# One block with the second experts' weights and twelve tiles' rows ahead, and logits with the gate as stationary operand

## The reference

```python
# layer 0 attention: Sim = e.w1 + d.w2 + (e*w3) d^T, softmax, and
#   hcq = concat(e, hq_hat, e*hq_hat, e*hc_hat) @ W_qv + b_qv
# layer 0 experts (8 of width 512, and 4 that give x back), on the normalised rows
logits = einsum('btd,ed->bte', x, gate_w) + expert_bias     # 12 experts
topk_logits, topk_idx = top_k(logits, 2);  topk_w = softmax(topk_logits)
h = silu(x @ w1[e].T);  y = h @ w2[e].T                     # per expert
# layer 1 attention: 4 heads of 64, softmax(q k^T * scale) v, @ Wo
# layer 1 experts (8 of width 1024)
logits = xf @ Wg                                            # 8 experts
comb = one_hot(top_idx) * softmax(top_vals) * alpha
y = gelu(layernorm(xf)*ln_w[e]+ln_b[e] @ fc1_w[e] + fc1_b[e]) @ fc2_w[e] + fc2_b[e]
```

## Time and profile before

| what | value |
|---|---|
| median of 3 runs | 962.05 us |
| the profiled execution, its own time | 967.79 us |
| its span, first to last instruction | 965.9 us |
| mean granted TensorE clock | 0.956 |
| TensorE busy | 894.5 us (93%) |
| VectorE, ScalarE, GpSimd busy | 562.0, 491.3, 431.3 us |
| DMA | 134.72 MB, mean 139 GB/s |

### The profile page before, as it was taken

How to read it: one execution, slowest core, us unless ns; L and a number is a source line. 1 busy time by engine, 2 the same in 40 slices (tenths; PEclk the granted TensorE clock), 3 DMA queues, 4 the chain that set the end, 5 groups by cost and what they waited for, 6 DMA issues and landing times. The chain is left out here.

```text
span 965.9 us, 19473 instructions
## 1 busy us (share of the span) xinstructions
PE 894.5 (93%) x6189; PEld 766.2 (79%) x6190; DVE 562.0 (58%) x1286; ACT 491.3 (51%) x1044; POOL 431.3 (45%) x374
## 2 busy tenths in 40 slices
PE   6899999868999998779999999988899999999995
PEld 4798989746899996557777777757499999999995
DVE  7875453485566675666566575554764454454452
ACT  5744141354444553475665665545655455455552
POOL 2474341004555573755363462300255555555543
PEclk9999999978999999789999999985999999999998
DMA  9721000275766746611010100019667666676662
GB/s 306 239 95 44 1 1 1 76 248 187 254 228 232 253 157 221 135 44 44 5 63 22 45 1 2 28 52 353 229 184 195 211 200 190 209 203 187 206 198 28
DMA packets 68593, 134.72 MB, mean 139 GB/s; under 512 B 8080, under 2 KB 50704, under 8 KB 63408
## 3 DMA queue, kind: packets, MB, share of 16 engines
q1 hardware_dynamic: 55184, 110.27, 33.4%
q0 software_dynamic: 13344, 23.63, 11.2%
HBM read 109.08 MB, written 21.64 MB: 135 GB/s over the span
## 5 line engine op out<-in xcount | busy, mean ns | idle before, releaser
L1901 PEld LDWEIGHTS d_hps<-d_xg_t,d_xw 128*128 128x128 f32 x1248 | 145.2, 192 | 2.4 <-DVE d_xg_t L2085 1.0
L1799 ACT ACTIVATE x<-d_hps,b 128x128 f32<-128x128 f32 x312 | 89.3, 368 | 113.1 <-PE d_hps L1901 112.9
L1901 PE MATMUL d_hps<-d_xg_t,d_xw 128*128 128x128 f32 x1248 | 145.5, 275 | 0.8 <-DVE d_xg_t L2085 0.8
L883 POOL TENSOR_SCALAR c_prob<-c_prob,c_rinv 128x1024 f32<-128x1024 f32 x64 | 72.4, 1150 | 109.4 <-DVE c_rinv L1338 109.0
L1911 PE MATMUL d_yps<-d_w,d_hid_hi 128*128 x312 | 115.2, 402 | 0.0
L1704 POOL DMA_INDIRECT out_x<-d_y,d_take_slot x39 | 63.1, 1619 | 99.1 <-DVE d_y L2122 89.6
L1331 DVE CUSTOM_DVE_ANT_0 c_prob<-c_sc,c_minf 128x1024 f32<-128x1024 f32 x64 | 75.8, 1221 | 36.6 <-PE c_sc L976 34.4
L2085 DVE TENSOR_SCALAR d_xg_t<-d_take,ln_w,ln_b 128x128 f32<-128x128 f32 x78 | 28.5, 406 | 93.4 <-PE d_take L1890 93.1
L1914 PE MATMUL d_yps<-d_w,d_hid_lo 128*128 x312 | 81.2, 281 | 0.0
L1901 PEld LDWEIGHTS b_hps<-b_xg_t,b_w 128*128 128x128 f32 x624 | 76.7, 195 | 3.6 <-issue 1.9
L989 PE MATMUL c_tp<-const,c_prob 128*128 128x128 f32 x512 | 70.5, 281 | 9.8 <-DVE c_pt L1343 5.2
(11 more groups left out here) (367 smaller groups left out, 2106.6 us busy)
## 6 DMA issues: line engine op xcount, KB each, us to landing
d_xw<-in_w SPq DMA_DIRECT2D x39, 1024.0 KB
b_w<-in_w SPq DMA_DIRECT2D x47, 512.0 KB, 7.6
d_w<-in_w SPq DMA_DIRECT2D x8, 1024.0 KB, 12.3
a_raw<-in_ctx_t SPq DMA_DIRECT2D x8, 512.0 KB, 7.0
a_raw<-in_ctx SPq DMA_DIRECT2D x8, 512.0 KB, 4.6
ybuf<-a_zero SPq DMA_DIRECT2D x2, 2048.0 KB, 12.5
k_stage<-in_ctx_t SPq DMA_DIRECT2D x12, 256.0 KB, 3.0
rows<-b_xn_all SPq DMA_DIRECT2D x1, 2048.0 KB, 12.6
```

The costliest lines, as they stand in the source:

```text
L883: nc.gpsimd.tensor_scalar(prob[w][:], prob[w][:], rinv[:, w:w + 1], 1.0, ALU.mult, ALU.mult).then_inc(s["prob_ready"], 1)
L1799: op = nc.scalar.activation(hid[q][:, h * FH + c, :], src[:, c, :], ACT.Gelu_apprx_tanh, bias=b1[:, ds(e, 1), h * FH + c])
L1901: mm = nc.tensor.matmul(hps[j % 2][h][:, c * P:(c + 1) * P], w1[j % WL][:, k, at:at + P], xg_t[j % 2][:, k, :], start=(k == 0), stop=(k == ...
```

## The change

- The last stage joins the block of the two before it, so that one block holds `experts(0)`, `attention1` and `experts(1)`, and one barrier less stands between them.
- Experts 2 and 3 of layer 1's w2 are loaded during the second attention and split there in halves: high on ScalarE after units (1,1), (1,7), (2,1), (2,7), low on GpSimd after units (1,2), (2,0), (2,2), (3,0).
- Experts 0 and 1 are loaded when the last batch's v is done, their high parts made on ScalarE at the attention's end and their low parts on GpSimd behind its last unit (`later_low`, two operations of 128x2048).
- Expert 4 is loaded after the last maxima. Then SyncE waits for twelve normalised tiles, sends their rows to DRAM, and only behind them loads experts 5, 6 and 7. The last four tiles' rows follow when all 16 are done.
- VectorE normalises tiles 0 to 4 before the last `keep_second`, tiles 5 to 11 behind the first `add_projection` of the last batch, and makes the last batch's statistics in two halves.
- The low parts of experts 4 and 5 are VectorE's, those of 6 and 7 TensorE's; none is left for behind the slots.
- In both layers the gate is the stationary operand of the logits, 256 rows at a time, and the logits land with experts on partitions; ScalarE copies four tiles of them (`keep_logits`), and TensorE turns them back (`turn_logits`). The warm matmuls of the pairs are gone, and the five ahead stay in layer 0 alone.
- In layer 0 the w2 loads share a semaphore by pairs of experts, so that `high(0)` waits for two experts' weights.
- Buffers are laid out anew and several semaphores are merged.

```diff
+EARLY_LOW = (2, 3)
+LATER_LOW = (0, 1)
+FREE_FIRST = 4
+LAST_LOW = (5, 6, 7)
+HIGH_ORDER = (0, 1, 4, 5, 6, 7)
...
@@ attention1, sync
+                else:
+                    sp.wait_ge(s["sum_p"], 2 * TB * (B - 1))
+                    for n in EARLY_LOW:
+                        m.load_w2(sp, n)
+            sp.wait_ge(s["v_done"], B * 4)
+            for n in LATER_LOW:
+                m.load_w2(sp, n)
             out_rows(B - 2)
             sp.dma_start(dram["out"][T * P:(T + 1) * P, :], m.x[:, 0, :]).then_inc(m.out_ready, 16)
+            sp.wait_ge(s["max_done"], B * UP * 2)
+            m.load_w2(sp, FREE_FIRST)
+            m.early_rows(sp)
+            sp.wait_ge(s["av_done"], B * 4)
+            for n in LAST_LOW:
+                m.load_w2(sp, n)
             out_rows(B - 1)
@@ attention1, gpsimd
                     normal(b, u)
+                    if (b, u) in EARLY_AT:
+                        m.early_low(pool, EARLY_AT.index((b, u)))
...
+            for n in LATER_LOW:
+                m.later_low(pool, n)
@@ attention1, scalar, end
             keep_first(B - 1, 7, 0)
+            root(0, B - 1, 21)
             keep_heads(B - 1, 2)
             keep_first(B - 1, 7, 1)
+            for n in LATER_LOW:
+                m.high(act, n)
             keep_heads(B - 1, 3)
-            root(0, B - 1, 21)
@@ attention1, vector, end
             keep_second(B - 1, 7, 0)
+            dve.wait_ge(s["v_done"], B * 4)
+            inverse_std(nc, m, dve, s["stat"], s["sqrt_done"], cols(0, B - 1), 15, 3)
+            m.early_normal(dve, 0, 5)
             keep_second(B - 1, 7, 1)
-            dve.wait_ge(s["x_bn"], 2 * B - 1)
-            variance(nc, m, dve, s["stat"], cols(0, B - 1), 15)
-            late_scale(0, B - 1, 15, 3)
             add_projection(B - 1, 0, xb)
+            m.early_normal(dve, 5, T - TB)
+            half_stats(0)
             add_projection(B - 1, 1, tp[1])
+            half_stats(1)
@@ experts
+    DVE_LOW, PE_LOW, DVE_LAST = ((0, 1, 2, 3), (4, 5), (6, 7)) if first else ((4, 5), (6, 7), ())
+    HIGH_AT = (1, 3, 5, 7) if first else (4, 5)
...
+        def high(act, e):
+            if first:
+                act.wait_ge(w2_in[e // 2], 32)
+            else:
+                act.wait_ge(w2_in[e], 16)
+            nc.scalar.activation(w2[:, e, :, 0, :], w2[:, e, :, 1, :].bitcast(F32), ACT.Copy).then_inc(s["w2_hi"], 1)
...
+        def later_low(pool, e):
+            pool.wait_ge(s["w2_hi"], high_count(e))
+            nc.gpsimd.tensor_tensor(w2[:, e, :, 1, :], w2[:, e, :, 1, :].bitcast(F32), w2[:, e, :, 0, :],
+                                    ALU.subtract).then_inc(s["w2_lo_pool"], 1)
+
+        def early_normal(dve, lo, hi):
+            for t in range(lo, hi):
+                normalise(nc, m, xn_all[:, t, :], t).then_inc(s["xn_dve"], 1)
+
+        def early_rows(sp):
+            sp.dma_start(gw[:], ...)
+            sp.dma_start(alpha[:], ...)
+            sp.wait_ge(s["xn_dve"], T - TB)
+            sp.dma_start(dram["rows"][0:(T - TB) * P, :] ..., xn_all[:, 0:T - TB, :]).then_inc(s["xn_out"], 16)
+            sp.dma_start(dram["rows"][T * P:(T + LANES) * P, :] ..., xn_all[:, 0:LANES, :]).then_inc(s["xn_out"], 16)
@@ experts, scalar
+            def keep_logits(group):
+                act.wait_ge(s["logit_done"], 2 * group + 2)
+                nc.scalar.activation(by_expert[:, group * 4 * P:(group + 1) * 4 * P], logit_t(group),
+                                     ACT.Copy).then_inc(s["logit_kept"], 1)
...
             for i in range(PAIRS):
                 ...
+                if i % 2 == 0 and i:
+                    keep_logits(i // 2 - 1)
                 if i == 2:
                     act.wait_ge(s["stat"], 7 if first else 6)
                     nc.scalar.activation(m.std[:, LAST], m.var[:, LAST], ACT.Sqrt, ...)
                 if i in HIGH_AT:
+                    high(act, DVE_LOW[HIGH_AT.index(i)])
+            keep_logits(PAIRS // 2 - 1)
@@ experts, tensor
             def logits(i):
+                group, at = i // 2, i % 2 * 2 * P
                 pe.wait_ge(s["xn_t"], i + 1)
-                for a in range(2):
-                    t = 2 * i + a
-                    for k in range(KD):
-                        mm = nc.tensor.matmul(lps[:, t * ne:(t + 1) * ne], xn_t[i % TPX][:, a, k, :], gw[:, k, :], ...)
+                if i % 2 == 0 and group >= 2:
+                    pe.wait_ge(s["logit_kept"], group - 1)
+                for k in range(KD):
+                    mm = nc.tensor.matmul(logit_t(group)[:, at:at + 2 * P], gw[:, k, :], xn_t[i % TPX][:, :, k, :], ...)
+            def turn_logits(group):
+                pe.wait_ge(s["logit_kept"], group + 1)
+                for a in range(4):
+                    t = 4 * group + a
+                    mm = nc.tensor.transpose(lps[:, t * ne:(t + 1) * ne], by_expert[:, t * P:(t + 1) * P], ident[0:ne, 0:ne])
...
-            warm(5, rank)
+            if first:
+                warm(5, rank)
...
+                if i + AHEAD < (PAIRS if first else PAIRS - AHEAD):
                     turn_pair(i + AHEAD)
+                if not first and i == PAIRS - AHEAD:
+                    for late in range(i, PAIRS):
+                        turn_pair(late)
                 logits(i)
-                warm(1, rank)
+                if i % 2 == 0 and i:
+                    turn_logits(i // 2 - 1)
+            turn_logits(PAIRS // 2 - 1)
...
-            for e in PE_LOW[:2]:
+            for e in PE_LOW:
                 low_out(e)
-                if e == (PE_LOW[1] if first else PE_LOW[0]):
+                if e == PE_LOW[1]:
                     value_parts()
```

More of the change, by code:

```diff
@@ L33 @@
 LANES = 3
+EARLY_LOW = (2, 3)
+LATER_LOW = (0, 1)
+FREE_FIRST = 4
+LAST_LOW = (5, 6, 7)
+ROUTED = {n: k + 1 for k, n in enumerate("load exp_in expert blk val slot g gate_at".split())}
+ACT_ROUTED = {n: k + 1 for k, n in enumerate("exp_ready val0_ready off_ready lane_act".split())}
+HIGH_ORDER = (0, 1, 4, 5, 6, 7)
 GATHERS = 6
@@ L1443, in vector @@
                 keep_second(b, 4, 1)
+                if not more:
+                    new_stats(b - 1)
                 both_maxima(b, 6)
@@ L1451, in vector @@
                 keep_second(b, 5, 1)
+                if not more:
+                    dve.wait_ge(s["x_bn"], 2 * B - 1)
+                    variance(nc, m, dve, s["stat"], cols(0, B - 1), 15)
                 both_maxima(b, 7)
@@ L1501, in experts @@
         c16 = lambda at, n: m.c16[:, at - C_ONES:at - C_ONES + n]
+        if not first:
+            xw = sb("xw", [P, T * D])
         w2 = sb("w2", [P, E, FC, 2, D], F32R)
@@ L1613, in run @@
+        if not first:
+            m.load_w2, m.high, m.early_high, m.early_low, m.later_low = load_w2, high, early_high, early_low, later_low
+            m.early_normal, m.early_rows = early_normal, early_rows
         def run(eng, step):
@@ L1940, in step @@
                     pe.wait_ge(s["w2_lo_act"], len(PE_LOW) * CH + 2)
+                    if not first:
+                        pe.wait_ge(s["w2_lo_pool"], 2 * len(EARLY_LOW) + len(LATER_LOW))
                 down(n, j, e)
@@ L2213, in build, with _ @@
-        with nc.cleanup_on_exit():
-            last = experts(nc, m, dram, 1)
-            with nc.Block() as block:
-                block.sync(last.sync)
-                block.tensor(last.tensor)
-                block.scalar(last.scalar)
-                block.vector(last.vector)
-                block.gpsimd(last.gpsimd)
+            with nc.Block() as block:
+                @block.sync
+                def _(sp):
+                    first.sync(sp)
+                    second.sync(sp)
+                    last.sync(sp)
+                @block.tensor
+                def _(pe):
+                    first.tensor(pe)
+                    second.tensor(pe)
+                    last.tensor(pe)
+                @block.scalar
+                def _(act):
+                    first.scalar(act)
+                    second.scalar(act)
+                    last.scalar(act)
+                @block.vector
+                def _(dve):
+                    first.vector(dve)
+                    second.vector(dve)
+                    last.vector(dve)
+                @block.gpsimd
+                def _(pool):
+                    first.gpsimd(pool)
+                    second.gpsimd(pool)
+                    last.gpsimd(pool)
```

240 lines of the change are left out of this document (123 added, 117 removed).

## The result

The change makes the kernel slower: 968.81 us (median of 20 runs, 966.66 to 973.82) against 961.88 (20 runs, 958.13 to 971.86), a ratio of 1.0076, 95% interval 1.0057 to 1.0095. The forecast was 960.5 with a range up to 967.5, so it missed low, by 8.3 us. The profiled execution of after took 967.74 us (span 966.0, mean granted clock 0.967).

A forecast was written before the change was run, and what follows sets the result against it. TensorE bounds layer 1's blocks; the second routing runs at half clock after the barrier's pause. -2.5 - 1.3 + 2.3 = -1.5 us takes 967.79 to 966.3; less 5.74 for the median, 960.5, range 950 to 967.5.

The forecast's parts named there:

- -2.5 - 1.3 + 2.3 = -1.5 us: Whole kernel: second routing 2.5 us earlier, its end to first `up` 1.3 shorter, first routing 2.3 later.
- the 5.74 us: Whole kernel: the median of the runs is 5.74 us below the profiled execution, taken off to reach 960.5.
- C: Second routing: start of VectorE's chain of choices, forecast to move from 670.74 to 668.2, 2.5 us earlier.
- Rival B: Second routing: most runs of before keep full clock there, so the change is +1.9 us, 964.0; chance 0.20.
- C without and with the collision: Second routing: chain of choices starts at 658.8, 11.9 us earlier, if VectorE isn't held; at 668.2 if it is.
- the collision: Ahead of second routing: VectorE's normalisings wait for GpSimd's 4.7 us differences, so tiles 5 to 11 end at 649.4.
- C to the first block: Layer 1, chain of choices to first `up`: 27.5 us against 28.8, 1.3 earlier, in layer 0's order.
- clock effect of 1.3: Layer 1's first block: 1.3 us from the clock after a pause, as in layer 0, counted before first `up`.
- The first routing: Layer 0: start of the choices at 202.2 against 199.88, 2.3 us later, bounds 1.0 and 4.8.
- pair's wait: First routing: high(0) waits for two experts' weights, half a megabyte more, 1.5 us.
- Costs taken at nothing: Second attention: ScalarE's and GpSimd's early halves fit into gaps at no cost; uncovered they'd cost 1 us each.

The follow-up runs named there:

- before at the median: The kernel before, unchanged, timed against itself and profiled again: 963.33 us, ratio 1.0011; the profiled execution took 961.91 us.
- Experiment 2: Kernel after, with the low parts of experts 0 and 1 made by VectorE and not GpSimd: 962.42 us, ratio to before 0.9979.
- experiment 5: Kernel after, with SyncE issuing the loads of experts 5 to 7 ahead of the rows: 964.74 us, ratio to before 1.0008.
- experiment 6: Kernel after, with low parts of experts 0 and 1 on VectorE and the first routing as before: 958.47 us, ratio to before 0.9945.
- experiment 3: Kernel after, with the first routing as it was before, layer 1 as after: 965.28 us, ratio to before 1.0019.
- experiment 4: Kernel after, with layer 1's experts in a block of their own again, so the barrier is back: 980.86 us, ratio to before 1.0159.

## Why the prediction was wrong

**The step that failed is the last one of the sum: "-2.5 - 1.3 + 2.3 = -1.5 us: the profiled execution's 967.79 becomes 966.3. The median of the runs is 5.74 lower, so 960.5."** In the frame of the profiled execution the forecast was 1.4 us from the trace of after (966.3 against 967.74). But the 5.74 us weren't a constant that both kernels carry. They lay mostly in the stage that the change rebuilds: between the two traces of before (5.9 us apart) the half clock makes the stretch from the last projection to C 8.95 us longer, of which 2.32 come back between C and `up`; the other stages together differ by 0.7 the other way. The change removes that stage's old form, and with it the part by which the profiled execution was slow. Taking the 5.74 off again counted it twice. The median of after is 1.1 us above its profiled execution, not 5.7 below. The runs show in place of -2.5 between projection and C, against before at the median, +6.46. That the sum came so near in the frame of the profiled execution is in part luck: -1.83 in the first attention, which the change doesn't touch, and +2.16 in layer 0's blocks and the second attention nearly cancel.

**Rival B** said this, with a chance of 0.20, and its 964.0 was still 4.8 us low, for three reasons. It guessed before's C at full clock as 665.0; it is 661.8. It let the new C gain 2.3 from the clock (665.9), but after's clock falls as well: 1.00 to 660.7, 0.50 from there to C. And it had the first routing 0.9 us too cheap. Against that stands C to `up`, 5.0 us shorter where it had 1.3; the other stages, which its sum left out, add 1.5.

**C without and with the collision.** The mechanism was right, link by link: both GpSimd operations of 4.5 us (forecast 4.7), seven tiles held 10.54 us, twelve tiles done, then rows, then expert 5, then ScalarE's wait. Last projection to C was forecast as 668.2 - 641.75 = 26.45 us and measured as 26.50. With the 3.47 us by which after's projection is later, high(5) was due at 663.7 and the last logits at 670.3; they came at 663.77 and 670.42. Only the fall of the clock was placed wrong: the forecast had it in the wait for expert 5, and it came before that wait, at 660.7, behind TensorE's waits for the copies that stand behind the square root and expert 4's high part. Experiments 2 and 5 show both links by taking them away. Without the collision the forecast had 658.8 - 641.75 = 17.1 us from the projection to C at full clock. Experiment 2 has 19.16 at a clock of 0.91, and experiment 6, with the same code there and a clock of 1.00, has 17.96. So about 1.2 us are the clock and 0.9 the forecast's own sum.

**C to the first block.** The forecast's -1.3 holds a clock effect of 1.3 that isn't in this stretch but in the first block behind it; without it the forecast is -2.6, and measured are -2.70 in the frame of the profiled execution and -5.02 in that of the median. The effect itself was forecast as 1.3 and measured as 1.5 (the first `up` takes 8.94 us, in the earlier trace rows 7.41). The new order is layer 0's, as forecast: C to the last slot is 20.58 us (forecast 20.4) and from there to `up` 5.55 (forecast 5.8). What I didn't see is that the rows of before stand behind all of w2 in SyncE's queue, so that with the earlier C the first gather waits for their landing (683.19, while `take_slot` was there at 681.57), the second takes 2.94 us, and TensorE waits 2.66 us for its rows ahead of `up`. In the profiled execution the half clock hid these waits. Two loads of w1 run beside the late gathers; whether they are a cause no run shows.

**The first routing.** Forecast +2.3 with bounds of 1.0 and 4.8, measured +3.19 and +3.09. The term was mis-sized: pair's wait 1.2 (forecast 1.5), form 2.0 to 2.3 (forecast 0.8). I had priced four copies of 0.5 us on ScalarE, and not that ScalarE stands before them for TensorE's logits.

**Costs taken at nothing.** The early halves do fit into the attention. The +0.41 us of the stage is no proof, since single traces differ by more; but in the 160 us that hold them, up to 25 us ahead of the last projection, TensorE is idle for 0.44 us in after and for 0.44 in both traces of before. The moved statistics aren't free, though: in the last 25 us it is idle for 1.6 us where before had 1.2. One operation on the way to the variance took 1.03 us, where its neighbours took 0.16 to 0.20, beside a GpSimd scaling, and the maximum stands behind it:

```profile
629.36 1.03 DVE L96 TENSOR_TENSOR diff<-bn 128x12 f32<-128x12 f32 x1
...
630.99 1.22 DVE L1363 CUSTOM_DVE_ANT_0 c_prob<-c_sc,c_minf 128x1024 f32<-128x1024 f32 x1
```

I take it for the same collision in small; no run took it away. Layer 1's blocks are 1.07 us longer; the first `up` is 0.6 of it (8.94 against 8.38), and I have no cause for the rest.

**The account.** By experiments 2 and 3 the collision is 6.4 us of the time and the first routing 3.5; without both, the change is faster than before by 0.55% (experiment 6). So the change without its two side effects is worth some 4 to 5 us, and these cost 10. How its parts (w2 ahead, rows ahead, no barrier) share the 4 to 5 us no run shows.

## What to carry to other kernels

Where the one trace at hand isn't from an execution at the median, don't subtract the difference from the sum. Find the stage in which it lies; if the change rebuilds that stage, the difference goes with it. Before giving GpSimd a long operation with two SBUF sources, look at what VectorE has to do beside it: here a 0.4 us operation waited for the whole 4.6 us, and whatever sits behind it in a DMA queue waits too. And a barrier waits for the queue that issues DMAs as well, which may be the last to arrive, as in experiment 4.

## What the runs showed of the hardware

- Behind the same pause of 3.27 us on TensorE the granted clock stayed at 0.50 until 680 in one execution of the kernel before; in another it fell only at 647.4 and was back at 1.00 at 650.8. One trace doesn't tell which is common; of 105 executions 33 had a mean clock of 0.960 or less.
- The issue of a load on SyncE took longer behind other transfers: three of a megabyte took 6.74 us (experiment 4) and 6.92 us (after) to issue behind the rows, 2.76 us ahead of them (experiment 5), and all eight of before 19.27 us.
- A VectorE normalising of 128x256, one source, 0.41 us alone, took 4.40 and 4.61 us beside GpSimd differences of 128x2048.
- One expert's difference of 128x2048 takes VectorE 2.29 us and GpSimd 4.56.
